# A GRU step whose gate products stream 32 columns instead of 8, with two unused matrix products at its end

## What is computed

```python
def step(h, xt):
    xr_t, xz_t, xn_t = xt
    r = jax.nn.sigmoid(xr_t + h @ w_hr.T + b_hr)
    z = jax.nn.sigmoid(xz_t + h @ w_hz.T + b_hz)
    n = jnp.tanh(xn_t + r * (h @ w_hn.T + b_hn))
    h_new = (1.0 - z) * n + z * h
    return (h_new, h_new)
```

## Time and profile before

| | us |
|---|---|
| median of 3 runs | 1589.59 (1588.03 to 1593.13) |
| profiled execution, its own time | 1583.21 |
| its span | 1581.5 |
| TensorE busy (matmuls) | 1348.3 |
| TensorE weight loads busy | 1015.0 |
| DVE busy | 1178.4 |
| ACT busy | 864.2 |
| POOL busy | 434.8 |

### The profile page before, as it was taken

One profiled execution on the slowest core, in us unless ns is written; L12 is line 12 of the kernel. 1 busy time (PEld: TensorE's weight loads), 2 busy tenths in 40 slices (PEclk: granted clock), 3 DMA queues, 4 the chain that ended last, 5 costly groups with the idle time before them and its releaser, 6 DMA issues. The chain is left out here.

```text
span 1581.5 us, 62097 instructions
## 1 busy us (share of the span) xinstructions
PE 1348.3 (85%) x25307; PEld 1015.0 (64%) x25322; DVE 1178.4 (75%) x5086; ACT 864.2 (55%) x2987; POOL 434.8 (27%) x818
## 2 busy tenths in 40 slices
PE   5888888888888888888888885679999999999886
PEld 4677777777777777777777774345556555655443
DVE  5778888888888888888888885666667767666485
ACT  3555444444444444444444442337777777777764
POOL 2101111111111111111111112544534544532364
PEclk6555555555555555555555555669999999999998
DMA  5200000000000000000000000294753852860001
GB/s 122 32 4 5 5 7 5 5 7 5 5 7 5 6 6 5 6 5 5 7 5 5 7 5 6 69 151 79 125 61 67 126 72 61 120 76 10 1 18 37
DMA packets 68930, 53.47 MB, mean 34 GB/s; under 512 B 12687, under 2 KB 68391, under 8 KB 68647
## 3 DMA queue, kind: packets, MB, share of 16 engines
q1 hardware_dynamic: 66470, 49.32, 18.7%
q10 hardware_dynamic: 2176, 0.20, 0.1%
HBM read 31.84 MB, written 15.47 MB: 30 GB/s over the span
## 5 line engine op out<-in xcount | busy, mean ns | idle before, releaser
L735 PE MATMUL PS<-GQ,W 128*128 128x8 f16 x12288 | 521.2, 169 | 137.6 <-DVE GQ L1079 124.6
L735 PEld LDWEIGHTS PS<-GQ,W 128*128 128x128 f16 x12288 | 447.7, 105 | 243.3 <-DVE GQ L1079 231.2
L966 ACT ACTIVATE RQ<-PS 128x16 f32<-128x16 f32 x512 | 101.5, 198 | 387.5 <-PE PS L735 387.3
L2424 DVE TENSOR_REDUCE MX<-PS 128x1 f32<-128x512 f32 (+3 forms) x352 | 219.6, 635 | 112.2 <-PE PS L1883 109.2
L2162 ACT ACTIVATE PT<-PS 128x512 f32<-128x512 f32 (+1 forms) x352 | 193.2, 566 | 114.5 <-PE PS L1899 110.0
L1070 DVE TENSOR_TENSOR_SCAN PS<-RQ,PS 128x64 f32<-128x64 f32 x512 | 151.3, 295 | 96.7 <-ACT RQ L966 83.8
L955 ACT ACTIVATE GB<-GQ 128x32 f16<-128x32 f16 x512 | 171.7, 335 | 0.8 <-DVE GQ L1084 0.8
L689 POOL TENSOR_TENSOR rt<-mv,eps 128x1 f32<-128x1 f32 x96 | 18.4, 192 | 512.2 <-DVE mv L1093 512.2
L766 PE MATMUL PS<-Y,V 128*128 128x32 f16 x2322 | 151.7, 204 | 0.0
L968 ACT ACTIVATE ZT<-PS 128x16 f32<-128x16 f32 x512 | 98.3, 192 | 89.6 <-PE PS L735 89.3
L1079 DVE TENSOR_TENSOR_SCAN GQ<-ZT,NT 128x48 f16<-128x48 f32 x512 | 132.2, 258 | 18.6 <-ACT NT L970 0.9
(11 more groups left out here) (401 smaller groups left out, 2843.3 us busy)
## 6 DMA issues: line engine op xcount, KB each, us to landing
QS<-q_parts SPq DMA_DIRECT2D x90, 128.0 KB, 10.8
KS<-k_parts SPq DMA_DIRECT2D x90, 128.0 KB, 13.0
q_parts<-PQ SPq DMA_DIRECT2D x16, 384.0 KB, 10.3
k_parts<-PK SPq DMA_DIRECT2D x16, 384.0 KB, 3.2
X<-XM SPq DMA_DIRECT2D x32, 64.0 KB
out_dram<-X SPq DMA_DIRECT2D x8, 256.0 KB, 2.3
XM<-in_L_attn_x_dram SPq DMA_DIRECT2D x16, 80.0 KB
s_hh<-in_L_attn_w_hh_dram SPq DMA_DIRECT2D x1, 768.0 KB, 5.4
```

The costliest lines, as they stand in the source:

```text
L735: return pe.matmul(bank[:, p, at:at + B], W[:, kc, w:w + P], state[:, kc, :, part], start=False, stop=True, skip_group_check=True)
L2424: dve.tensor_reduce(MX[:, g % 2, heads[0]:heads[-1] + 1, NT - 1 - it], p_x[:, k % 2, 0:len(heads) * w].rearrange("p (a w) -> p a w", w=w), ...
```

## The change

WIDE = U x B = 32 becomes the room that one step has in a bank of the reset or the update gate, where it had B = 8. `product` streams the 8 state columns four times (a broadcast with stride 0) and writes 32 columns; only the first 8 of them are read. `inject` writes its 32 columns as four runs of 8, to the first 8 columns of each step's 32, and ACT reads the gates there. Of a bank's 512 columns, 256 are then in use, where it was 64. Columns 256 to 511 receive the two unused products: at the end of each step's own work, behind `inject` and ahead of the pieces of `schedule`, TensorE multiplies one block of W1 with 256 columns of W1, once into the reset gate's bank and once into the update gate's, of the side that is not in use. Nobody reads the result, and no wait and no signal goes with it. The number of products rises by 2 a step, 1024 in all; no other engine has an instruction more or less, and none changes its place.

```diff
@@ -450,6 +450,7 @@
         SLOTS = GS
         RG = 3
         LAG = 2
+        WIDE = U * B
         ctx = ExitStack()
         with ctx:
             STx = sb(ctx, "STx", [P, 6])
@@ -731,8 +732,9 @@
                 def product(gate, p, k, state, mc, kc, W, part):
                     bank, g = gates[gate]
                     w = (HC * g + mc) * P
-                    at = (mc * U + k) * B
-                    return pe.matmul(bank[:, p, at:at + B], W[:, kc, w:w + P], state[:, kc, :, part],
+                    at = (mc * U + k) * WIDE
+                    return pe.matmul(bank[:, p, at:at + WIDE].rearrange("p (r b) -> p r b", b=B), W[:, kc, w:w + P],
+                                     state[:, kc, :, part].unsqueeze(1).to_broadcast([P, WIDE // B, B]),
                                      start=False, stop=True, skip_group_check=True)
 
                 def candidate_w2(p, k, state, mc, kc):
@@ -751,19 +753,19 @@
                     for bank, which, bias, chunk in gates_at:
                         for mc in range(HC):
                             if which is None:
-                                o = bank[:, p, mc * U * B:(mc + 1) * U * B]
+                                o = bank[:, p, mc * U * WIDE:(mc + 1) * U * WIDE].rearrange("p (u w) -> p u w", u=U)[:, :, 0:B]
                             else:
                                 o = candidate(p)[:, :, mc, :, which].rearrange("p u b i -> p u (b i)")
                             if bias is not None:
                                 n = 2 * U * B if which == HIGHS else U * B
                                 pe.matmul(o, brow[:, (bias + mc) * P:(bias + mc + 1) * P],
-                                          ones3[:, 0:n] if which is None else ones3[:, 0:n].rearrange("p (u n) -> p u n", u=U),
+                                          ones3[:, 0:n].rearrange("p (u n) -> p u n", u=U),
                                           start=start and mc == 0, stop=False, skip_group_check=True)
                             if chunk is not None:
                                 w = slice((chunk + mc) * P, (chunk + mc + 1) * P)
                                 for V, Y in ((V1, Y1), (V2, Y1), (V1, Y2)):
                                     y = Y[:, rows]
-                                    pe.matmul(o, V[:, w], y if which is None else y.rearrange("p (u b) -> p u b", u=U),
+                                    pe.matmul(o, V[:, w], y.rearrange("p (u b) -> p u b", u=U),
                                               start=False, stop=False, skip_group_check=True)
                         start = False
                 HIGHS, THIRD = slice(1, 4, 2), slice(2, 3)
@@ -801,6 +803,9 @@
 
                     rows = columns(pe, first * B + (s // U + 1) * (U * B), U * B)
                     inject((r_in, z_in, n_in, xn_in)[k], 1 - p, rows, k < 3)
+                    for bank in (pR, pZ):
+                        pe.matmul(bank[:, 1 - p, HC * U * WIDE:2 * HC * U * WIDE], W1[:, 0, 0:P], W1[:, 1, 0:HC * U * WIDE],
+                                  start=False, stop=True, skip_group_check=True)
 
                 def inputs(j, s):
                     if s == 0:
@@ -958,7 +963,7 @@
                 def steps(first, s, ring):
                     p, k = s // U % 2, s % U
                     n = first + (s + 1) if isinstance(first, int) else act.snap(first + (s + 1))
-                    now = lambda bank: bank[:, p, 0:U * NSTEP].rearrange("p (c u b) -> p c u b", c=HC, u=U)[:, :, k, :]
+                    now = lambda bank: bank[:, p, 0:HC * U * WIDE].rearrange("p (c u w) -> p c u w", c=HC, u=U)[:, :, k, 0:B]
                     member = lambda x, i: x[:, :, i].rearrange("p (c b) -> p c b", c=HC)
                     if isinstance(first, int) and first == 0 and s == 0:
                         act.wait_ge(hr_start.sem, 5)
```

## The result

The kernel with the change takes 1569.45 us (median of 4 runs, 1565.32 to 1570.91), the one before 1590.87 (4 runs, 1588.03 to 1593.13). The ratio is 0.9862, with a 95% interval of 0.9836 to 0.9888: 21 us faster by the medians. The forecast was 8 us faster. The time lies in the stated range, but outside the 1577 to 1588 us of the forecast's own case: only a rival's part of the range reaches down to it.

What follows compares the result with a forecast made beforehand. The update gate's chain was taken to bind each recurrence step, at half TensorE clock, the candidate's having 0.02 us of slack. A gain of 512 x 0.015 = 8 us from the median 1589.6 gave 1582 us; range 1566 to 1606.

Steps and rivals of the forecast that it cites:

- the forecast's own case: Whole kernel: full clock held, pace about 25 ns, 8 us faster, 1577 to 1588 us; chance 0.42.
- I take nothing of that back: Mean recurrence step: its 0.02 us above the plain step, from DVE and POOL work, was taken to stay.
- this wait binds already: a faster TensorE wins nothing in the 14 products ahead of it: Reset products on the state's low part wait for DVE L1084, starting 0.08 us behind it; no gain from the 14 before.
- The clock: TensorE in the recurrence: half clock was to rise to full in the first steps and hold.
- the rival of the clock that does not stay: Recurrence: clock falls in steps carrying fewest columns, 0 to 14 us slower, 1590 to 1604 us; chance 0.22.
- The stretches that the forecast set side by side: TensorE outside the recurrence: clock fell after 1030.9 to 1034.3 us, filled 0.35; stayed full around 1538 despite 2.38 us idle.
- The pace at full clock: TensorE's small products: 27 ns each at half clock, taken as 25 at full, bounded by 13.4 and 27.
- The rival of a pace that follows the clock: TensorE's small products at 13 to 20 ns: 16 to 26 us faster, 1564 to 1574 us; chance 0.15.
- The plain step: One ordinary recurrence step, 1.81 us: was to gain 15 ns, giving 1.79 us.
- The candidate's chain: Reset products, ACT L966, DVE L1070, ACT L970 to the next state: ends 4 to 5 ns later, using part of 20 ns slack.
- The update gate's chain: Last of 32 products, ACT L968, DVE L1075 to the next state: binds, and gains 17 x 1.8 - 10 = 20 ns.
- The unused pair is hidden: Two 256-column products ending each step: 0.43 us at half clock, 0.22 at full, covered by TensorE's slack in plain steps.

## Why the prediction was right on the clock and too small in its sum

Two steps of it failed: "I take nothing of that back", on what the mean step takes above the plain one, and "this wait binds already: a faster TensorE wins nothing in the 14 products ahead of it". The recurrence gained 17.5 us, not 8.

- **The clock** rose in the second step and stayed, as taken. The experiments show that this was no safe thing: with no unused products, a good quarter of the columns less, it was full in half of the recurrence. That is the rival of the clock that does not stay, in a neighbour of this kernel. The stretches that the forecast set side by side pointed the right way.
- **The pace at full clock**, taken as 25 ns, is 25 ns, for 8 columns (in the kernels with narrow gates: the same starts) and for 32. The Trainium skill's floor of about 25 ns (TensorE: Matmul & The Clock Gate, section "Wait — 56ns, not 53.3ns?") is what these traces show. The rival of a pace that follows the clock had forecast the right time, 1564 to 1574, by a wrong mechanism, and it is its part of the range that the time fell in.
- **The plain step** was to gain 15 ns and gained 23. The step that failed is the wait for the low part. In the earlier trace rows the six products around it take 0.30 us, 5 x 27 + 169 ns: there is no gap, and the first low product, 80 ns behind L1084, went out at TensorE's own pace. So it was in 481 of 511 steps of the trace. In most of the others, step 4 of a group (counted from 0) as in the earlier trace rows, L1084 ended later and TensorE waited. All 18 products from the state on were on the path.

  With the change TensorE does wait, in 504 of the 511: the first low product starts 58 ns behind L1089, 22 ns earlier than before (431 against 453 ns behind the state). The wait then puts 39 ns between it and the next one, where it was 27, so that the last of the four starts at 519 ns instead of 533. The wide product's result comes 11 ns later, as forecast to within 1. The candidate's chain was to reach ACT 4 to 5 ns later and reaches it 2 to 3 ns earlier (735 ns behind the state against 737 to 738, medians over the plain steps); with its slack of some 20 ns used up, that is the 23. The update gate's chain ends 26 ns earlier, forecast 20. The difference, 512 x 0.008, is 4 us.
- **"I take nothing of that back"**, on the mean step's 0.02 us above the plain one, is the other. The cause of most of it was two engines meeting. The update gate's chain is 26 ns earlier now (ACT L973 starts 1085 ns behind the state, where L968 started at 1111), so that in the long steps DVE starts ahead of POOL's addition, where it was the other way round, and a wait of 0.30 became one of 0.13. It is shown by the runs that hold the addition back: what is left to win from it is 7.7 us before the change and 3.5 after, so the change gained 4.2 us there without any step of the forecast. The rows of the long steps give 28 x 0.157 = 4.4 us. The steps 3 to 5 of a group lost another 46 ns of their excess together, 1.3 us over all groups. In step 4 L1081 took 251 ns on average instead of the 231 of the other steps, so that L1084 was late; with the change it takes 231 there too. Why, and what the other two waited for, was not tried apart.
- **The sum**: 511 x 0.023 = 11.8 us of pace and slack, 4.4 us from the long step, 1.3 us from steps 3 to 5, together 17.5, as measured. The forecast of 8 us has the first of these, two thirds of it, and nothing else.
- **The unused pair is hidden**, as forecast, with 0.3 us left at full clock in a plain step (452.82 to 453.13). ACT's other addresses and the runs of 8 columns cost nothing that can be seen.

## What to carry to other kernels

In this kernel a chain of small products had its clock raised by making the products wider at no cost in pace, and by filling slack with products that nobody reads; but the clock must hold in the emptiest stretch, for where it does not, the filling is what slows the steps at half clock. Keep the product that ends a chain narrow. Before calling a wait binding, look for the gap: products that go out at their usual pace behind it have not waited. And look for pairs of DVE and POOL instructions that start within some ten ns of each other: which comes first can be worth more than the pace, and a wait that moves POOL's into a gap settles it.

## What was not expected of the hardware

- An addition on POOL with two tensors from SBUF and a DVE instruction that reads two tensors from SBUF meet here at DVE's cost. In the 26 long steps of before where it started 6 to 12 ns behind POOL, DVE took 0.48 instead of 0.18 us, and ended about when POOL did. With the change it starts 25 to 33 ns ahead in 27 of them (20 in the lines shown, which are rounded), takes its 0.18, POOL its usual 0.46, and DVE's scan of two tensors, which comes 0.19 us into POOL's addition, takes 0.39 instead of 0.26 us. The Trainium skill (GPSIMD Engine Reference, section 1, Specifications) states that POOL shares its way into SBUF with DVE and contends with DVE instructions of two SBUF inputs. The trace agrees, and adds that some 10 ns in the order of the two starts decide how much DVE pays. In one step of before DVE started only 4 ns behind POOL and still took its 0.18, so the border is not exactly at equal starts.
- A TensorE product that waited for a semaphore adds about 20 ns ahead of the next one at half clock (first to second product 47 ns apart, then 27) and 14 at full clock (39, then 25). At the wait for the low part the same gap is there only where TensorE waited: 27 ns in the steps of before that did not, some 46 in the 27 that did, some 39 in 504 of 511 steps of the change.
- The stages behind the recurrence differ by 6 us between two executions of the same kernel (619.5 and 625.2 us), with the places where their clock falls. A single profiled execution is no base for a difference of that size.
